# A router front moved into attention's last turns, and two casts of a scan moved to later slots

## The reference

```python
x = x + 0.5 * L0_ffn(layernorm(x))      # layer 0: 8 experts, top 2, 128x128 each
x = x + L0_attn(layernorm(x))           # layer 1: one head, cos/sin features, softmax
x = x + 0.5 * L0_ffn(layernorm(x))      # layer 2: the same experts again ("FFN 2")
x = x + 0.5 * L1_ffn(layernorm(x))      # layer 3: 16 experts, attention inside
x = x + L1_attn(layernorm(x))           # layer 4: conv, delta, selective scan, gate ("the scan")
x = x + 0.5 * L1_ffn(layernorm(x))      # layer 5
```

## Time and profile before

| | us |
|---|---|
| median of 3 runs (1643.15, 1646.88, 1647.20) | 1646.88 |
| the profiled execution | 1653.55 |
| its span | 1651.7 |
| TensorE busy | 1408.3 |
| VectorE busy | 1150.0 |
| ScalarE busy | 528.7 |
| GpSimd busy | 533.2 |
| attention, window 126 to 272 | 146.0 |
| between attention's last addition and FFN 2's first unit, 272 to 307 | 35.0, of it TensorE busy 11.25 at a granted clock of 0.51 |
| scan, window 744 to 1290 | 546.0, of it VectorE busy 458.1 |

### The profile page before, as it was taken

One profiled execution on the slowest core, in us unless ns is written; L12 is line 12 of the kernel. 1 busy time (PEld: TensorE's weight loads), 2 busy tenths in 40 slices (PEclk: granted clock), 3 DMA queues, 4 the chain that ended last, 5 costly groups with the idle time before them and its releaser, 6 DMA issues.

```text
span 1651.7 us, 21271 instructions
## 1 busy us (share of the span) xinstructions
PE 1408.3 (85%) x7178; PEld 1019.0 (62%) x7178; DVE 1150.0 (70%) x2582; ACT 528.7 (32%) x1015; POOL 533.2 (32%) x446
## 2 busy tenths in 40 slices
PE   2887877595999999987888888978978599999997
PEld 2884544595899999962333323323323489999996
DVE  3785663485577777541998989889899557777753
ACT  2203444200122222214555545555454012222221
POOL 1150000001000000002899788788899100000000
PEclk9997998797999999987899999999989689999999
DMA  4650000562333332301332322222332333333330
GB/s 151 204 193 1 1 0 1 193 218 103 104 103 104 104 103 104 104 0 34 97 101 73 94 88 86 88 87 82 91 99 67 103 103 110 110 110 110 110 110 13
DMA packets 93162, 155.11 MB, mean 94 GB/s; under 512 B 11703, under 2 KB 21374, under 8 KB 92926
## 3 DMA queue, kind: packets, MB, share of 16 engines
q1 hardware_dynamic: 93054, 153.76, 28.6%
HBM read 150.31 MB, written 3.41 MB: 93 GB/s over the span
## 4 chain that ended last, share of the span: by engine, by line
PE 65%; DVE 15%; issue 11%; ACT 3%; POOL 3%; DMA 2%; DVEq 0%; POOLq 0%; SPq 0%; ACTq 0%
PE bank L1090 21%; PE bank L1093 7%; PE bank L1205 6%; PE bank L952 5%; DVE hs L1558 3%; PE bank L1144 3%; PE bank L983 3%; PE bank L1050 2%; DVE both L1550 2%; PE bank L1035 2%; DVE xe L1558 2%; PE bank L1102 2%; PE bank L1032 2%; PE bank L992 2%; PE bank L1042 1%
## 5 line engine op out<-in xcount | busy, mean ns | idle before, releaser
L1090 PE MATMUL bank<-wqkv_sb,xe 128*128 128x192 f32 x2048 | 370.3, 333 | 10.4 <-DVE xe L1501 10.0
L1090 PEld LDWEIGHTS bank<-wqkv_sb,xe 128*128 128x128 f32 x2048 | 340.0, 194 | 21.7 <-DVE xe L1501 15.2
L1205 PE MATMUL bank<-both,ident 128*128 128x512 f32 x512 | 261.3, 636 | 42.7 <-DVE both L1550 36.1
L569 POOL TENSOR_TENSOR rstd<-ve,half_neg 128x4 f32<-128x4 f32 x32 | 37.6, 1174 | 730.5 <-DVE ve L1259 730.5
L853 ACT ACTIVATE bank<-dt,A 128x512 f32<-128x512 f32 x256 | 175.3, 688 | 193.4 <-DVE hs L1558 110.0
L1205 PEld LDWEIGHTS bank<-both,ident 128*128 128x128 f32 x512 | 94.8, 199 | 182.1 <-DVE both L1550 89.7
L1558 DVE TENSOR_TENSOR_SCAN xe<-bank,both 128x512 f32<-128x512 f32 x128 | 152.7, 1210 | 41.1 <-ACT bank L853 41.1
L601 POOL TENSOR_TENSOR both<-du,prT 128x512 f32<-128x512 f32 x128 | 161.0, 1269 | 26.5 <-DVE xe L1558 15.5
L601 POOL TENSOR_TENSOR both<-du,prob 128x512 f32<-128x512 f32 x128 | 160.7, 1270 | 22.2 <-DVE hs L1558 17.8
L1558 DVE TENSOR_TENSOR_SCAN hs<-bank,both 128x512 f32<-128x512 f32 x128 | 154.3, 1212 | 9.7 <-ACT bank L853 9.7
L952 PE MATMUL bank<-exp_sb,xe 128*128 128x128 f32 x1024 | 128.7, 284 | 26.5 <-DVE xe L1384 25.9
(11 more groups left out here) (256 smaller groups left out, 1990.7 us busy)
## 6 DMA issues: line engine op xcount, KB each, us to landing
dt<-w_rows SPq DMA_DIRECT2D x128, 256.0 KB, 4.1
du<-w_rows SPq DMA_DIRECT2D x128, 256.0 KB, 4.9
prob<-bc_dram SPq DMA_DIRECT2D x64, 256.0 KB, 3.3
prT<-bc_dram SPq DMA_DIRECT2D x64, 256.0 KB, 3.3
dt<-g_dram SPq DMA_DIRECT2D x32, 256.0 KB, 6.1
du<-g_dram SPq DMA_DIRECT2D x32, 256.0 KB, 6.8
g<-g_dram SPq DMA_DIRECT2D x32, 256.0 KB, 7.2
u<-g_dram SPq DMA_DIRECT2D x32, 256.0 KB, 6.8
```

What stands on the lines that cost most here:

```text
L569: pool.tensor_tensor(rstd[:], ve[:], half_neg[:, 0:NT], ALU.pow).then_inc(ln_rstd, 1)
L1090: m = pe.matmul(bank[4 + j // 2][:, (j % 2) * 3 * HD:(j % 2 + 1) * 3 * HD], x_e, wqkv_sb[:, e, :], start=(e == 0 and j % 2 == 0), stop=(e ...
L1205: pe.matmul(bank[4 + k % NH][:], ident[:], hc[k % HRING], start=False, stop=(SUM_RANK[k] == sums_of(k // UNITS, k % NH))).then_inc(hc_used, 1)
```

## The change

Two edits in one.

**The front of FFN 2's first group** is taken out of layer 2's loops and made by `ffn(2, 1, early=True)`, whose steps the attention layer calls. VectorE makes the 16 statistics and the variance in `main(4)` and `gnmr` at the head of `main(5)`, and the whole choice of experts in `main(7)`, before it waits for the values of that turn. GpSimd makes `grstd` before the `rstd` of sequence 6. ScalarE normalises sequences 0 and 1 after the third and fourth Exp of `main(5)`, 2 and 3 in `main(6)`, into four buffers `xn_early` of their own (so no wait for transposes), and makes the four copies to `gxT` after the four Exps of `main(7)`. TensorE transposes and scores in `main(7)`: transposes after each score tile, scores in bank 4, the last two between the value matmuls. A new semaphore `gxn_made` counts these tiles, and `xn_made` counts only the others.

**In the scan** ScalarE's casts go from slots 1 and 3 to 3 and 6. TensorE's second computation of the rest goes from slot 2 to 3, the first half of the second convolution from 3 to 4, z1 from 12 to 13, the output from 7 to 8; VectorE's addition of the output goes from 10 to 11.

```diff
-FRONT7 = {"xT": -7, "dlt": -4, "conv0": -3, "conv1": 5, "z0": 11, "z1": 12, "res0": 17, "res1": 20}
-OUT7 = 7
+FRONT7 = {"xT": -7, "dlt": -4, "conv0": -3, "conv1": 5, "z0": 11, "z1": 13, "res0": 17, "res1": 20}
+OUT7 = 8
...
+        xn_early = [t[:].rearrange("p (j c) -> p j c", j=NT) for t in hs[0:GROUP]]
...
             def norms(layer):
                 for b in range(NB):
+                    if layer == 1 and b == NB - 2:
+                        group_rstd(1, 0)
                     rstd_of(layer * NB + b)
...
-            def ffn(layer, r):
+            def ffn(layer, r, early=False):
                 def front(G):
                     def normed(s):
                         g = layer * NB + GROUP * G + s
                         act.wait_ge(gnmr_made, seen(2 * r + G + 1))
-                        act.wait_ge(xT_ps, seen(g - 1))
+                        if not early:
+                            act.wait_ge(xT_ps, seen(g - 1))
+                        to = xn_early[s] if early else xn_odd if s % 2 else xn
...
+                        if early and s == 0:
+                            act.wait_ge(frac_made, seen(4 * NB))
...
+                    ahead = GROUP if early else 2
+                    for s in range(GROUP + ahead):
+                        if s >= ahead:
+                            turned(s - ahead)
+                        if s < GROUP:
+                            normed(s)
+                        yield
...
+                group = ffn(2, 1, early=True)
                 def main(b, par, ahead):
                     act.wait_ge(acc_ps, seen(b))
                     for k in range(NT):
...
                         step(ahead, k, (0,))
+                        if b == NB - 1 or b >= NB - 3 and k >= 2:
+                            next(group)
                     finish(ahead)
                 overlapped(front, main)
+                finish(group)
...
-                steps = on_clock(front, (-10, -6, -3, -1, 1, 3, 7, 12, 13, 15, 16, 18, 22))
+                steps = on_clock(front, (-10, -6, -3, -1, 3, 6, 7, 12, 13, 15, 16, 18, 22))
...
                 def main(b, par, ahead):
                     for k in range(NT):
...
                         step(ahead, k, (0, 1))
+                        if b == NB - 1:
+                            next(group)
                     pe.wait_ge(acc_used, seen(layer * NB + b))
                     pe.wait_ge(v_made, seen(b + 1))
                     for k in range(NT):
+                        if b == NB - 1 and k in (1, 2):
+                            next(group)
                         pe.wait_ge(p_made, seen(NT * b + k + 1))
...
-                steps = on_clock(front, (-7, -5, -4, -3, -1, 2, 3, 5, 11, 12, 17, 20), back, (OUT7,))
+                steps = on_clock(front, (-7, -5, -4, -3, -1, 3, 4, 5, 11, 13, 17, 20), back, (OUT7,))
...
                 def main(b, par, ahead):
+                    if b == NB // 2 + 1:
+                        next(group)
                     for _ in range(3):
                         next(ahead, None)
+                    if b == NB // 2:
+                        for _ in range(5):
+                            next(group)
+                    if b == NB - 1:
+                        finish(group)
                     dve.wait_ge(acc_ps, seen(b + 1))
...
-                steps = on_clock(front, (-13, -11, 1, 9, 15, 18, 20, 24), back, (4, 5, 10))
+                steps = on_clock(front, (-13, -11, 1, 9, 15, 18, 20, 24), back, (4, 5, 11))
```

## The result

| | before | changed |
|---|---|---|
| median of 7 runs, us | 1647.2 | 1654.7 |
| lowest to highest, us | 1643.15 to 1651.72 | 1649.61 to 1658.53 |
| profiled execution, us | 1653.55 | 1649.61 |
| ratio of the times, 95% interval | 1 | 1.0043 [1.0025, 1.0061] |

The changed kernel is slower by 0.43%, where 1639.3 us and a gain were forecast. One thing has to be seen before the traces are read: the profiled execution of before lies above all seven of these runs, and the one of the changed kernel is the fastest of its seven. By the two profiles the change gains 3.9 us; by the medians it loses 7.5. What the traces show stage by stage stands, but the total is the medians'.

A forecast was written before the change was run, and what follows sets the result against it. VectorE bounds the scan; attention to FFN 2 is one serial chain with hardly anything beside it. -19.0 + 4.7 + 2.2 + 2.0 + 2.5 = -7.6 us from 1646.88 gives 1639.3 us, own range 1635 to 1643, eight in ten 1632 to 1646.

The forecast's parts named there:

- Part 1: Attention's last turn: first scores to logits falls from 33.6 to 14.6 us, gain 19.0; the following 13.6 us stay.
- Part 2: Turns 4 and 5 on VectorE: statistics cost 3.7 us, waiting for GpSimd 1.0; cost 4.7 us in all.
- Part 3: Turns 5 and 6 on ScalarE: normalising makes the sines late; turn 5 is covered, turn 6 costs 2.2 us.
- Part 4: Clock in attention's turn 5: TensorE's wait of 7.7 us brings a fall costing 2.0 us, bounds 0 and 2.7.
- Part 5: The scan: moved casts cost 0 us per steady sequence, bounds 0 and +1; the first sequence costs +2.5 us.
- the bound given, 5.32: In the scan, the most a clock fall costs: the 5.32 us VectorE waits where TensorE is behind today.
- The first sequence: The scan's first sequence: the later cast delays everything behind it by 3.4 us; taken as +2.5, bounds 0 and 3.4.
- the guess that the slow stretch would fall into the wait: Scan's first sequence: part of TensorE's slow stretch may fall into the wait, so +2.5 us was taken, bound 3.4.
- the rival of the other side: Scan: idle time moved to slots 3 and 4 costs the clock, 3.0 us in each of six sequences; 1657.3 us, chance 0.07.

The follow-up runs named there:

- casts_only: The kernel of before with only the scan's casts and the TensorE rest computations that hang on them moved later; 1677.13 us, ratio 1.018.
- casts_swap: Late casts alone on the kernel of before, but with conv1's first half put into TensorE's gap ahead of the second rest computation; 1656.79 us, ratio 1.0062.
- scan_only: The kernel of before with the change's scan slots alone, the router front left as before; 1676.5 us, ratio 1.0175.

## Why the prediction was wrong

**Part 1, right.** Forecast 14.6 and 13.6 us, in the trace 14.66 and 13.42. The stretch from the first scores to the first `xe` went from 306.29 - 259.10 = 47.2 to 28.1 us: 19.1 gained, 19.0 forecast.

**Part 2, right.** `gnmr` waited 0.98 us for GpSimd (forecast 1.0). TensorE waited 7.53 us where 7.7 were forecast.

**Part 3, right in mechanism.** Turn 5's lateness was covered (turn 6 lasts 260.55 - 243.51 = 17.04 us). In turn 7 the first scores start 266.74 - 260.55 = 6.19 us after the start of the values before them, against 259.10 - 254.63 = 4.47 before: 1.7 us, forecast 2.2.

```profile
254.63 3.74 PE L992 MATMUL bank<-vext,both 128*128 128x130 f32 x32
```

**Part 4, right.** The turn is 23.44 - 17.05 = 6.4 us longer; less what part 2 cost in the trace, 7.53 - 2.97 = 4.6, that leaves 1.8 for the clock (0.50 in the window above), forecast 2.0. It did not come again in turn 6.

Together -19.1 + 6.4 + 1.7 = -11.0 us, forecast -10.1, and measured by itself -10.9.

**Part 5, wrong, and all of the miss.** The step that failed is the sentence "The idle time is moved, not lengthened: **0 us**, bounds 0 and +1 a sequence". Its timing was nearly right: the wait of 1.46 us went away and one of 1.90 us came in slot 4. Wrong was the conclusion that idle time of about the same length costs the same wherever it stands; the step priced the clock at nothing. Before, TensorE has two short gaps, then unbroken work from 977.59 to 984.04, 6.4 us, and then the wait of 1.46 us:

```profile
975.65 1.13 PE L1205 MATMUL bank<-both,ident 128*128 128x512 f32 x2 [0.40 <-DVE both L1550]
977.36 0.39 PE L1193 MATMUL bank<-bcT,pick 96*128 96x512 bf16 x1 [0.59 <-DVE both L1550]
977.59 1.88 PE L1205 MATMUL bank<-both,ident 128*128 128x512 f32 x4
```

With the late casts the 1.90 us follow the same two gaps with only 2.74 us of work between, the sums at 989.58 in casts_only's trace above, and there the clock falls, in most sequences. What TensorE then does at 1.2 GHz is all ahead of a spread of C for which VectorE has no slack. A fall was priced in the rival at 3.0 us a sequence. The place itself gives 3.1 when a sequence has it in full, 18.6 us in six; with the first sequence's 3.5 that is 22.1 of the 30 us that the scan is longer, and the rest lies in waits that other traces have without this fall. By the whole 30 us it is 5 us a sequence; the bound given, 5.32, holds.

The first sequence was forecast at +2.5 with a bound of 3.4, and is 5.07 - 1.39 = +3.7. The guess that the slow stretch would fall into the wait did not come true: TensorE was slow from 780.37 to 788, the granted clock is 0.50 to 0.51 there.

So the rival of the other side, with a chance of 0.07 and 1657.3 us, was what happened, and 1654.7 was measured. That its number comes so near is in part luck: it counts six falls at 3.0 us, and the changed kernel's trace has four. Its chance was too low for a stated reason, "the idle time is hardly longer than the present 1.46 us", that looked at one gap's length alone. The Trainium skill ("TensorE: Matmul & The Clock Gate", HAM oscillation) has the clock fall by waits between bursts of matmuls, and the prediction used it for attention's turn alone. Asked of this moved wait as well, it would have spoken for this rival, and the traces agree with it here: 0.50 behind the 1.90 us. The length of a single wait doesn't decide it in this case: 1.90 us in the scan, and 1.38 in casts_swap, were followed by a fall, while the 2.97 us of a steady turn of attention mostly weren't.

Two readings in the prediction were loose, and no term hangs on them. Slice 19 has VectorE at one tenth and is not yet the scan's steady part, and slices 4 to 9 have it at three to eight tenths, not four to seven.

**How the 30 us of the scan became 19 in the whole change.** Shown: the loss depends on what precedes the scan, since 1.8 us of delay raise it by some 11. Shown too: the shorter scan of the changed kernel's profile is one with four falls and not six. But these four account for 509.6 - 495.9 = 13.7 us only, and that execution lies 5.1 us under its kernel's median. So the usual execution of the changed kernel loses more than this trace shows, and of it there is no trace. Not shown is why the time of one program is nearly the same in nearly all its runs (scan_only: five runs at 1674.87 to 1677.13 us and one, the profiled one, at 1661.22 with four falls). The Trainium skill ("TensorE: Matmul & The Clock Gate", Part 1) says that the point isn't tied to the program. The runs agree in that one kernel has both times, and speak against it in that the other is so seldom. This stays open. So does what exactly about the place lets the clock fall: that the gap is the cause is shown by filling it, that the two short gaps ahead of it have a part in it is only argued, and casts_swap shows a fall without them close by.

## What to carry to other kernels

A wait that moves on TensorE is not free because it keeps its length: look at how much slack the work behind it has if it runs at 1.2 GHz, and price that before you call the move free. Measure the parts of a change by themselves before you accept or drop it as a whole: here a gain of 11 us and a loss of 19 to 29 lay in one edit. And set a profiled execution beside the median before two traces are subtracted: these two differ by -3.9 us, and the kernels by +7.5.

## What the runs showed of the hardware that was not expected

A wait of 1.90 us on TensorE, behind gaps of 0.40 and 0.59 us, brought the granted clock to 0.50, in four to six of six equal places, and two matmuls of no use in that gap kept it at 1.00 and saved some 27 us in 1677. Waits of 1.46 and 1.38 us in the same place, ahead of `D*u`, had no fall behind them in before and one in four of six sequences in casts_swap. And 1.8 us of delay ahead of the scan made the kernel some 11 us slower; its profiled scan is 526.6 us long where the changed kernel's, the fastest of its seven runs, is 509.6.
